# Mixed-precision 3x3 convolution on one core: bands of 8, 8, 4 and 8 row pairs, images prepared two ahead, and GpSimd forming two sums of the fast band

## What is computed

```
pooled = x.reshape(B, C, H // 8, 8, W // 8, 8).mean(axis=(3, 5))
m = pooled >= 0.05          # then repeated 8 x 8 to the image's size: mask
x_high = jnp.where(mask, x, EPS)
x_low = jnp.where(mask, EPS, x)
y_high = _conv(_quant_act_uint(x_high, act_scale_high, 8), _quant_weight_per_oc(w_high, 8))
y_low = _conv(_quant_act_uint(x_low, act_scale_low, 4), _quant_weight_per_oc(w_low, 4))
return y_high + y_low
```

## Time and profile before

| what | value |
|---|---|
| device time, median of 3 runs | 711.26 us (710.82 to 713.17) |
| the profiled execution | 710.8 us, of which the span of the trace is 709.0 us |
| PE busy in the span | 649.0 us, 92% |
| DVE busy | 593.7 us, 84% |
| ACT busy | 469.7 us, 66% |
| POOL busy | 10.0 us, 1% |
| mean granted clock of TensorE | 0.997 of full speed |
| data moved | 104.07 MB, 147 GB/s |

### The profile page before, as it was taken

One profiled execution on the slowest core, in us unless ns is written; L12 is line 12 of the kernel. 1 busy time (PEld: TensorE's weight loads), 2 busy tenths in 40 slices (PEclk: granted clock), 3 DMA queues, 4 the chain that ended last, 5 costly groups with the idle time before them and its releaser, 6 DMA issues.

```text
span 709.0 us, 11076 instructions
## 1 busy us (share of the span) xinstructions
PE 649.0 (92%) x3714; PEld 350.3 (49%) x3714; DVE 593.7 (84%) x956; ACT 469.7 (66%) x460; POOL 10.0 (1%) x30
## 2 busy tenths in 40 slices
PE   0699999999999999999999999999999999999996
PEld 0355554555555555545555554555555555555553
DVE  4987899888889888889888889888889988888963
ACT  3768667667667666766666766766766766766742
POOL 2300000000000000000000000000000000000000
PEclk9999999999999999999999999999999999999999
DMA  6234324434324434423444422443432443432122
GB/s 248 92 136 183 122 118 170 181 136 181 142 114 153 181 136 181 156 115 136 181 153 164 175 113 120 181 171 146 181 121 111 176 181 136 181 141 114 63 91 92
DMA packets 14553, 104.07 MB, mean 147 GB/s; under 512 B 1872, under 2 KB 1872, under 8 KB 10576
## 3 DMA queue, kind: packets, MB, share of 16 engines
q1 hardware_dynamic: 14256, 103.95, 38.5%
q10 hardware_dynamic: 288, 0.00, 0.0%
HBM read 52.56 MB, written 51.38 MB: 147 GB/s over the span
## 4 chain that ended last, share of the span: by engine, by line
PE 67%; DVE 26%; issue 3%; DMA 1%; ACT 1%; DVEq 1%; ACTq 0%
PE psum L317 67%; DVE plane_h L593 7%; DVE ybuf L656 5%; DVE ybuf L645 3%; DVE rowsum_h L611 2%; DVE upper L639 2%; DVE outer_l L623 2%; DVE inner_l L628 1%; DMA act_scale_h<-act_scale_high 1%; DVE pooled L566 1%; DVE rowsum_l L611 1%; DVE lower L639 0%; ACT wT_h L437 0%; ACT wT_l L437 0%; DVEq L592 0%
## 5 line engine op out<-in xcount | busy, mean ns | idle before, releaser
L462 ACT ACTIVATE psum<-psum,ratio 128x1176 f32<-128x1176 f32 (+1 forms) x128 | 165.4, 1292 | 179.5 <-PE psum L317 179.3
L317 PE MATMUL psum<-plane_l,wT_l 128*128 128x392 f16 x1164 | 219.6, 337 | 32.0 <-DVE ybuf L645 20.5
L317 PE MATMUL psum<-plane_h,wT_h 128*128 128x392 f16 x1164 | 219.5, 337 | 0.0
L317 PEld LDWEIGHTS psum<-plane_l,wT_l 128*128 128x128 f16 x1164 | 107.2, 96 | 138.5 <-DVE ybuf L645 32.4
L317 PEld LDWEIGHTS psum<-plane_h,wT_h 128*128 128x128 f16 x1164 | 112.2, 96 | 91.1 <-issue 1.6
L593 DVE TENSOR_TENSOR plane_l<-clipped_l,mask_l 128x1792 f16<-128x1792 f16 x64 | 62.3, 974 | 84.0 <-ACT mask_l L429 81.1
L656 DVE SCALAR_TENSOR_TENSOR ybuf<-psum,out_scale_h,shared 128x392 f32<-128x392 f32 x194 | 112.2, 618 | 10.1 <-ACT shared L469 8.7
L566 DVE TENSOR_REDUCE pooled<-xbuf 128x28 f32<-128x1792 f32 x64 | 111.2, 1777 | 0.0
L469 ACT ACTIVATE shared<-psum,bias,out_scale_h 128x392 f32<-128x392 f32 x128 | 86.2, 674 | 32.7 <-PE psum L317 32.7
L422 ACT ACTIVATE rounded_l<-xbuf,inv_act_l 128x1792 int16<-128x1792 f32 x64 | 101.9, 1592 | 7.7 <-DVE neg_q_eps_h L517 7.7
L422 ACT ACTIVATE rounded_h<-xbuf,inv_act_h 128x1792 int16<-128x1792 f32 x64 | 102.4, 1600 | 0.0
(11 more groups left out here) (78 smaller groups left out, 311.8 us busy)
## 6 DMA issues: line engine op xcount, KB each, us to landing
y<-ybuf SPq DMA_DIRECT2D x64, 784.0 KB, 3.3
xbuf<-x SPq DMA_DIRECT2D x31, 1568.0 KB, 7.6
xbuf<-x SPq DMA_DIRECT2D x1, 896.0 KB, 7.9
xbuf<-x SPq DMA_DIRECT2D x1, 672.0 KB, 10.1
wraw_l<-w_low SPq DMA_DIRECT2D x1, 576.0 KB, 5.7
wraw_h<-w_high SPq DMA_DIRECT2D x1, 576.0 KB, 8.9
act_scale_l<-act_scale_low ACTq DMA_DIRECT2D x1, 0.5 KB, 5.9
act_scale_h<-act_scale_high ACTq DMA_DIRECT2D x1, 0.5 KB, 8.2
```

The source lines that it names most:

```text
L317: last = nc.tensor.matmul(out, wT[k][:, mat, :], moving(k, p, band, row, dx), start=(k == "l" and j == 0), stop=(j == len(parts) - 1), ski ...
L462: nc.scalar.activation(banks, banks, ACT.Identity, scale=ratio[:, 0:1]).then_inc(s_scaled, 1)
```

## The change

1. **Bands.** 8, 8, 4 and 8 row pairs in place of 7, 7, 7, 7: matmuls of 448, 448, 224 and 448 columns. Band 3, the fast one, grows. The halves of the store follow (32 and 24 rows). The number of matmuls is the same.
2. **Two ahead.** While image n is multiplied, ACT rounds image n+2 and DVE sums and chooses its blocks; ACT expands the masks of n+1 at the start of image n. `rounded` and `mask` get two buffers each. Loads of x are issued one image earlier. Clipping, masking and row sums take a whole image in one instruction where there were two. The order of DVE's body is new.
3. **The fast band's sums.** ACT scales M1 and M2 of the low product before M0 and M3, and then also moves M2 out of PSUM (`second`). POOL forms `upper` and `lower` from `shared` and `second`. DVE keeps the two final rows.
4. **Start.** Both activation scales come in one transfer, the first on SP's queue (before: two on ACT's). The first part of image 0 is 24 rows in place of 32. PE does band 0's high product before band 1's low product in the first image, and the work of DVE and ACT there is reordered.

```diff
+    BAND = ((0, 8), (8, 8), (16, 4), (20, 8))
+    BANDS = len(BAND)
+    N_MAX = 8 * W
+    assert N_MAX <= 512 and sum(count for _, count in BAND) == PAIRS
...
-    CUT = (0, 4, BY)
+    CUT = (0, 3, BY)
...
+        mask = {k: [sb(f"mask_{k}{p}", [P, BY, W], F16) for p in range(2)] for k in "hl"}
+        shared = [sb(f"shared{s}", [P, N_MAX], F32) for s in range(2)]
+        second = sb("second", [P, N_MAX], F32)
...
             load_after(0, 0)
+            load_after(0, 1)
...
                 store(i, p, 0)
                 if load:
-                    load_after(i + p, 1 - p)
+                    load_after(i + 1, p)
                 store(i, p, 1)
...
+            def halves(n, band):
+                g = BANDS * n + band
+                pool.wait_ge(s_shared, g + 1)
+                pool.wait_ge(s_second, fast_index(n, band) + 1)
+                if not (early(n) and band == FAST[0]):
+                    pool.wait_ge(s_out, 2 * (g - BANDS) + 2)
+                for to, op, ready in ((upper, ALU.subtract, s_upper), (lower, ALU.add, s_lower)):
+                    nc.gpsimd.tensor_tensor(to[:, 0:columns(band)], shared[band % 2][:, 0:columns(band)],
+                                            second[:, 0:columns(band)], op).then_inc(ready, 1)
...
                     products("l", p, band, "M1")
+                    if not (early(n) and band == FAST[0]):
+                        pe.wait_ge(s_second, fast_index(n, band))
+                    products("l", p, band, "M2").then_inc(s_low_inner, 1)
                     pe.wait_ge(s_out, 2 * g - 3)
-                    products("l", p, band, "M2")
                     products("l", p, band, "M0")
                     pe.wait_ge(s_out, 2 * g - 2)
                     products("l", p, band, "M3").then_inc(s_low, 1)
...
+                    pe.wait_ge(s_scaled_inner, fast_index(n, band) + 1)
                     products("h", p, band, "M1").then_inc(s_high, 1)
-                    products("h", p, band, "M2")
+                    products("h", p, band, "M2").then_inc(s_high_second, 1)
...
+                if fast(n, band):
+                    act.wait_ge(s_low_inner, fast_index(n, band) + 1)
+                    scale_banks(first + 2, 2, band).then_inc(s_scaled_inner, 1)
+                    act.wait_ge(s_low, g + 1)
+                    scale_banks(first, 2, band).then_inc(s_scaled, 1)
...
+                if fast(n, band):
+                    act.wait_ge(s_high_second, fast_index(n, band) + 1)
+                    nc.scalar.activation(second[:, 0:columns(band)], psum[:, BANK[band % 2]["M2"], 0:columns(band)],
+                                         ACT.Identity, scale=out_scale["h"][:, 0:1]).then_inc(s_second, 1)
...
-                if after:
-                    quantise("l", *ahead, 0)
-                low_scaled(n, 0)
...
+                if ahead > 0:
+                    masks(n + 1, 1 - p)
+                if ahead > 1:
+                    quantise("l", i + 1, p, 0)
+                low_scaled(n, 0)
+                if ahead > 1:
+                    quantise("l", i + 1, p, 1)
                 low_scaled(n, 1)
                 shared_tile(n, 0)
-                if after:
-                    quantise("h", *ahead, 0)
+                if ahead > 1:
+                    quantise("h", i + 1, p, 0)
                 shared_tile(n, 1)
-                if first_image(n):
-                    turned_weights("l", 2)
-                if after:
-                    quantise("h", *ahead, 1)
+                if ahead > 1:
+                    quantise("h", i + 1, p, 1)
                 low_scaled(n, 2)
-                if after:
-                    act.wait_ge(s_chosen, n + 3)
-                    masks(n + 1, 0, BY)
                 low_scaled(n, 3)
                 shared_tile(n, 2)
...
+                if ahead > 0:
+                    clip("l", m, mp)
+                    clip("h", m, mp)
+                    apply_mask("l", m, mp)
+                    apply_mask("h", m, mp)
+                    row_sums("l", m, mp)
+                if not early(n):
+                    dve.wait_ge(s_stored[p], 32 * i)
+                out_rows(n, p, 0)
+                if ahead > 0:
+                    row_sums("h", m, mp)
                 out_row(n, p, 1, 0)
+                if ahead > 0:
+                    differences("l", m, mp, 3)
                 out_row(n, p, 1, 1)
-                if after:
-                    apply_mask("l", m, mp, 0)
-                    clip("h", m, 1)
-                    apply_mask("l", m, mp, 1)
-                    row_sums("l", m, mp, 0)
-                    apply_mask("h", m, mp, 0)
-                    row_sums("l", m, mp, 1)
-                    differences("l", m, mp)
-                out_row(n, p, 2, 0)
-                out_row(n, p, 2, 1)
-                if after:
-                    apply_mask("h", m, mp, 1)
-                if fast(n, 3):
-                    if after:
-                        row_sums("h", m, mp, 0)
-                    fast_rows(n, p, 3)
-                else:
-                    out_row(n, p, 3, 0)
-                    if after:
-                        row_sums("h", m, mp, 0)
-                    out_row(n, p, 3, 1)
-                if after:
-                    row_sums("h", m, mp, 1)
-                    differences("h", m, mp)
+                if ahead > 0:
+                    differences("h", m, mp, 3)
+                if ahead > 1:
+                    pool_blocks(i + 1, p)
+                    choose(n + 2)
+                out_rows(n, p, 2)
+                out_rows(n, p, 3)
```

More of the change, by code:

```diff
@@ L85, in conv_program @@
         chosen = sb("chosen", [P, BY * BX], F16)
[L86 to L89, removed]
+        mask = {k: [sb(f"mask_{k}{p}", [P, BY, W], F16) for p in range(2)] for k in "hl"}
+        shared = [sb(f"shared{s}", [P, N_MAX], F32) for s in range(2)]
+        second = sb("second", [P, N_MAX], F32)
+        upper = sb("upper", [P, N_MAX], F32)
+        lower = sb("lower", [P, N_MAX], F32)
         outer_taps = {k: sb(f"outer_taps_{k}", [P, 3, C], F16) for k in "hl"}
@@ L312, in products @@
             def products(k, p, band, tile):
-                out = psum[:, BANK[band % 2][tile], 0:N]
+                out = psum[:, BANK[band % 2][tile], 0:columns(band)]
                 parts = [(row, mat + dx, dx) for row, mat in PRODUCTS[tile] for dx in range(3)]
@@ L324, in low @@
                 new = not (first_image(n) and band < 2)
+                wait_prepared(s_rowsum["l"], n, band)
+                if new:
+                    pe.wait_ge(s_shared, g - 1)
                 if fast(n, band):
@@ L413, in quantise @@
                 if first_image(n):
+                    part = elements(q)
                     if q == 0:
@@ new lines, in differences, with y_rows, tile, by_rows @@
+                nc.vector.tensor_tensor(inner[k][band][p][:, :].rearrange("p (t w) -> p t w", w=INNER_PITCH),
+                                        d1, d2, ALU.subtract).then_inc(s_diff[k], 1)
+            def y_rows(p, band, e):
+                t0, count = BAND[band]
+                return rows(ybuf[p], (2 * t0 + e) * W, 2 * W, count)
+            def tile(band, name):
+                return psum[:, BANK[band % 2][name], 0:columns(band)]
+            def by_rows(flat):
+                return flat.rearrange("p (t w) -> p t w", w=W)
@@ L641, in fast_rows @@
-                for e, tile, scale, part, ready in ((0, "M0", out_scale["h"], upper, s_upper),
+                f = fast_index(n, band)
+                for e, name, scale, part, ready in ((0, "M0", out_scale["h"], upper, s_upper),
                                                     (1, "M3", neg_out_scale, lower, s_lower)):
```

342 lines of the change are left out of this document (190 added, 152 removed).

## The result

| | before | after |
|---|---|---|
| median of the runs | 711.04 us (710.68 to 713.17, 4 runs) | 664.66 us (663.03 to 667.19, 4 runs) |
| profiled execution, span | 710.8, 709.0 us | 663.03, 660.9 us |
| PE, DVE busy | 649.0, 593.7 us | 635.6, 553.4 us |

The ratio is 0.9345, with an interval of 0.9306 to 0.9384: 46.4 us less, where 664.3 us was forecast.

A forecast was written before the change was run, and what follows sets the result against it. PE was the bound, its 21.11 us per image set by a circle over the mask. Steady part -46.1, image 31 -1.55, tail +0.3, start +0.3 sum to -47.0 us: 663.8 profiled, forecast 664.3 us, own range 660 to 669.

The forecast's parts named there:

- The bound, and the circle: PE bounds; PE's band 2 low product, ACT's scaling, mask, DVE's masking and output rows, PE again set 21.11 us per image.
- Columns: PE's matmuls: 44,352 columns per image against 44,688, taking an image without pauses from 19.66 to 19.52 us.
- U: Time of each of POOL's two sums, `upper` and `lower`: 1.0 us taken, ends 0.55 and 3.7.
- E: The end of an image's last product on PE, when the next image starts; DVE's last fast row forecast at E + 2.6.
- Slack: DVE's output rows before PE's bank deadlines: 1.7 us at next image's A, 1.65 at M3, 2.1 at B.
- U under 1.8: Condition for PE not pausing: each POOL sum shorter than 1 + 1.65 / 2 = 1.8 us.
- Rival 2: GpSimd (POOL) becomes the bound and is slower: at sums of 3.7 us, period 23.3 us, time near 778; chance 0.05.
- Rivals 1 and 3: Rival 1: some waits stay, 669 to 705 us, chance 0.14. Rival 3: the circle only moves, 706 to 713 us, 0.04.
- Rival 4: PE's granted clock falls a few per cent when running without pause: 675 to 695 us; chance 0.03.
- Tail: After the last product: last row 2.6 us behind instead of 2.0, last store perhaps 0.3 less; net +0.3 us.
- Start: First image: fast band's transposes at 38 to 40, image 1 at 49.7 to 51.5 us; +0.3, between -4 and +2.

The follow-up runs named there:

- equal bands: The changed kernel with four equal bands of 7 pairs in place of 8, 8, 4 and 8: 669.88 us, ratio 0.9405.
- late POOL: The changed kernel with two more GpSimd sums of 448 elements per image on unread tiles ahead of `upper`: 681.08 us (one run).
- late mask: The changed kernel with ACT expanding the masks behind the scaling of band 1 instead of first in the image: 716.77 us (one run).
- weights first: The changed kernel with DVE forming the fast band's weights, in the first image, ahead of clipping image 1's h part: 660.46 us; 659.91 us in a later set.

## Why the prediction was right

- **The bound, and the circle.** Right, and shown: the mask put behind the second scaling, and nothing else, gives 716.77 us (one run, far outside the scatter) with pauses at A of band 2 and at M3. The equal bands show that the columns are not needed for the gain.
- **Columns.** 19.52 us forecast, 19.573 measured. The base of 19.66 was itself 0.03 low, since 2.59 and 2.06 are rounded rows; the equal bands ran at 19.69. The rest is in the fixed part: 198 ns for 448 columns in bands of 15 matmuls and 100 for 224 are 11 and 7 ns over their columns at 2.4 GHz, not 9 for both (the fast band's 196 is 9 over). Over 29 images the steady part gave 44.5 us instead of 46.1; image 31 gave 1.5, as said.
- **U.** 1.0 us forecast between 0.55 and 3.7; 1.14 measured, with starts 1.09 apart. The end of the fast rows, E + 2.6, became E + 2.9.
- **Slack.** 1.65 and 2.1 us forecast at M3 and at B, 1.8 and 1.8 measured; the next image's A, wanted from band 2's first row, had 1.7 and has 2.0. That M3 came out so near is in part luck: the fast rows end 0.3 us later than forecast, and DVE's work from there to band 1's last row is 10.4 us instead of 10.85 (the merged instructions had been counted at nothing). The list was not complete: the first fast row, wanted by A of band 1 (1.7 us of slack, found by the late POOL), and band 0's first row, wanted by A of band 2 (2.4, found by the late mask), are missing. Neither mattered for the forecast. The condition "U under 1.8" stands, since a longer U hits the first fast row only once and M3 twice; but a delay ahead of both sums hits the first fast row soonest.
- **Rival 2, POOL as the bound.** Its mechanism is real: 2.2 us more on POOL costs 0.5 per image. So is the contention, when a sum is placed beside the clips. The change has neither.
- **Rivals 1 and 3.** No pause in the steady part, no new circle.
- **Rival 4.** Not in the steady part: from 60 to 640 us the granted clock is 1.00 in both profiles. Over the span it was 0.988 to 0.996 in the four runs; the profiles show slow matmuls in the start, where the forecast did not reckon with them.
- **Tail.** +0.3 forecast. The last row ends at 657.45, 2.8 us behind the last product, and 3.45 us follow: 6.3 in place of 5.7, so +0.6.
- **Start.** The term that was mis-sized: +0.3 forecast, -2.7 measured in this profile (image 2 starts at 67.44, before at 70.11). The text gave the range of -4 to +2 and took a value from the side where the scales' lead is lost. The lead was 6.4 us at the first product (12.95 against 19.35, "up to 4" in the forecast), and 2.9 of it arrived at the transposes (36.46, forecast 38 to 40). In the second profile the transposes start at 39.00, image 1 at 50.41 and image 2 at 69.99, -0.1: there the forecast (38 to 40, 49.7 to 51.5, +0.3) holds. So the term has no one value; what it left out is that the start depends on the clock of each execution. Fast weights behind the clip that waits for ACT, which the forecast saw, make a pause of 4.16 us in both profiles, and behind it the clock fell in both.

The parts in sum: -44.5 - 1.5 + 0.6 - 2.7 = -48.1 us of span, 709.0 to 660.9. Against the forecast's -47.0 two misses of 1.6 and 3 us with opposite signs partly cancel. The medians differ by less, 46.4 us, since the starts of single executions differ, as told below. That 664.66 lies only 0.4 from 664.3 is thus luck to the size of these misses; the mechanism, and the steady part within 4%, are not.

## What to carry to other kernels

When an engine with idle time is late, look for the wait that closes a circle through the bound engine, and move the waited-for step a whole round ahead; then list every deadline of every shared buffer with its slack, the first reader's as well as the last's. Count moved work, and a helper engine's relief, only as far as they exceed that slack: DVE 1.1 us late, or with 41 us more to do over the whole run, changed nothing here; 2.2 us late on POOL or 3.5 on the mask did. Sizes that shorten a circle lose most of their worth once the circle is gone, so don't add up two edits that were measured apart.

## What the runs showed of the hardware

The start scatters with TensorE's clock. In the profiled execution with the sums on DVE, the first high products behind a pause of 0.97 us ran at half pace:

```profile
22.25 1.28 PE L359 MATMUL psum<-rowsum_h,wT_h 128*128 128x448 f16 x3 [0.97 <-ACT psum L511]
23.32 4.68 PE L359 MATMUL psum<-plane_h,wT_h 128*128 128x448 f16 x12
```

Twelve matmuls take 4.68 us where the steady part takes 2.55 (4.48 us from the group's start to the next, so 373 ns for 448 columns, the pace of 1.2 GHz); the window from 20 to 30 us has a granted clock of 0.66, and image 1 starts at 52.28. The same group in the changed kernel's profile, behind the same pause of 0.97 us, ran at full pace, with 1.00 in that window, and image 1 starts at 47.87. The changed kernel's second profile:

```profile
20.00:30.00 10.00, 7.76 (x39) 3.51 (x39) 8.43 (x9) 7.14 (x10) 1.45 (x3) 0.83 0.45 161
```
```profile
50.41 0.74 PE L359 MATMUL psum<-rowsum_l,wT_l 128*128 128x448 f16 x3
```

So one program's start differs by some 2.5 us between executions, and its 4 or 5 runs by 2.7 to 4.2. The level after a pause is 1.2 or 2.4 GHz: behind the pause of 4.16 us, 12 matmuls of 224 columns took 2.34 us instead of 1.37.

The granted clock of a window does not show all of it. In the changed kernel's first profile the window from 10 to 20 us has 1.00, and yet these matmuls, the first product of all, are slow:

```profile
14.03 3.80 PE L359 MATMUL psum<-plane_l,wT_l 128*128 128x448 f16 x12
```

The two profiles of the changed kernel tell where the scatter comes from. The first product starts at 12.95 and 12.99 us, the first high product at 21.54 and 22.61, band 1's low product at 24.51 and 27.05: there the whole 2.54 us has been lost. The stretch behind the pause of 4.16 us, to the high product of band 2, takes 6.07 us in both, some 1.6 more than at full pace; it costs time, but makes no difference between the two. The early delay arrives whole at image 1, and the rows show the way: ACT scales band 1 at 27.67 and 30.22, DVE's clip behind ACT's roundings starts at 32.68 and 35.22, and the fast band's weights stand behind the clip. With the weights first the clock is low early too (0.83 from 20 to 30 us in its second profile, 1.00 in its first; band 1's low product 1.6 us apart), but DVE forms the weights at 31.99 and 32.24, and image 2 starts only 0.26 us apart (64.89 and 65.15). So by these rows the new order narrows the scatter because an early delay no longer passes through the clip, and saves the slow stretch besides. The clock alone was not varied.

An idle bracket on PE understates what a wait costs: 0.36 us stood for 0.53 per image with POOL late, and 0.95 + 0.42 for 1.72 with the mask late, because the pipelined matmuls ahead of the pause reach into it in the rows.
